# One-hot blocks of layers 0 and 3 on ScalarE, one counter step per tile's sum, a third bank for layer 3's queries, and groups of one tile at a layer's end

## What is computed

```python
# layer 0 (four heads of 64; layer 2 alike, without elu; layer 1 one head, returns h + att @ node)
Wh = (h @ W).reshape(n, heads, d)
e  = leaky_relu(s_i[:, None, :] + s_j[None, :, :], 0.2)     # s_i, s_j: Wh times two halves of a
e  = where((adj == 0)[:, :, None], -inf, e)
out = elu(einsum('ijh,jhd->ihd', softmax(e, axis=1), Wh))
# layer 3 (attention with q, k, v)
scores = einsum('hnd,hmd->hnm', q, k) / 8 + (edge.T - 1) * 10000
ctx = einsum('hnm,hmd->hnd', softmax(scores, axis=-1), v)
```

## Time and profile before

| | us |
|---|---|
| median of 3 runs | 2181.08 (2172.83 to 2183.22) |
| the profiled execution | 2191.25 |
| span of the profile | 2189.4 |
| first part, to layer 0's gathers | 272 |
| layer 0, first gather to layer 1's first | 272 to 778 |
| layer 1 | 778 to 1244 |
| layer 2 | 1244 to 1712 |
| layer 3 | 1712 to 2189 |

### The profile page before, as it was taken

One profiled execution on the slowest core, in us unless ns is written; L12 is line 12 of the kernel. 1 busy time (PEld: TensorE's weight loads), 2 busy tenths in 40 slices (PEclk: granted clock), 3 DMA queues, 4 the chain that ended last, 5 costly groups with the idle time before them and its releaser, 6 DMA issues.

```text
span 2189.4 us, 24682 instructions
## 1 busy us (share of the span) xinstructions
PE 1404.7 (64%) x8310; PEld 1025.4 (47%) x8310; DVE 1550.8 (71%) x3408; ACT 577.5 (26%) x1038; POOL 1294.8 (59%) x1299
## 2 busy tenths in 40 slices
PE   3655223676676625666767437777888477777776
PEld 2434122555555414444555334554555265655565
DVE  3768897888888735555565256766776388888887
ACT  6777350222222201222222102222222111111111
POOL 0000077777776067777776277777772577777771
PEclk9555556778778758878788568988889789888988
DMA  9997134444443034444443134444542577777771
GB/s 374 404 366 249 14 99 118 113 120 116 116 115 100 15 93 108 112 112 112 112 111 100 51 105 128 139 138 136 138 138 87 182 225 226 218 212 212 216 216 58
DMA packets 151027, 328.57 MB, mean 150 GB/s; under 512 B 31210, under 2 KB 62832, under 8 KB 150896
## 3 DMA queue, kind: packets, MB, share of 16 engines
q0 software_dynamic: 71680, 213.24, 35.8%
q1 hardware_dynamic: 61552, 92.57, 11.7%
q10 hardware_dynamic: 17664, 21.12, 2.8%
HBM read 294.93 MB, written 31.90 MB: 149 GB/s over the span
## 4 chain that ended last, share of the span: by engine, by line
POOL 31%; DVE 24%; PE 19%; issue 16%; ACT 6%; DMA 2%; SPq 1%; ACTq 0%; DVEq 0%; POOLq 0%
POOL s_gb L749 31%; PE ps L1691 8%; DVE s_gb L1428 6%; PE ps L1607 4%; PE ps L1645 3%; DVE s_F L1366 2%; DVE s_F L1364 2%; ACT s_a L781 2%; DVE s_ST L1252 2%; DVE s_S L1407 2%; PE ps L1656 1%; DVE s_sc L1352 1%; PE ps L1589 1%; DMA s_adj<-in_adj_dram 1%; DVE s_tmp L1348 1%
## 5 line engine op out<-in xcount | busy, mean ns | idle before, releaser
L749 POOL DMA_INDIRECT s_gb<-s_tab,s_ji x1280 | 1290.6, 1008 | 600.2 <-issue 384.7
L1691 PE MATMUL ps<-s_gb,s_S 128*128 128x260 f32 (+1 forms) x2560 | 704.0, 435 | 30.5 <-DVE s_gb L1428 23.7
L1691 PEld LDWEIGHTS ps<-s_gb,s_S 128*128 128x128 f32 x2560 | 552.2, 222 | 132.0 <-DVE s_gb L1428 26.2
L1428 DVE TENSOR_TENSOR s_gb<-s_gb,ps 128x1024 f32<-128x1024 f32 (+1 forms) x288 | 291.4, 1035 | 1.2 <-ACT ps L946 1.2
L1607 PE MATMUL ps<-s_wx,s_hT 128*128 128x264 f32 (+2 forms) x512 | 224.9, 575 | 83.7 <-ACT s_tb L887 42.7
L1656 PE MATMUL ps<-s_ident,s_sc 128*16 128x128 f32 (+1 forms) x384 | 79.6, 367 | 230.4 <-DVE s_sc L1327 229.6
L1645 PE MATMUL ps<-s_qs,s_ST 128*128 128x256 bf16 x960 | 156.9, 328 | 43.4 <-DVE s_tmp L1348 29.5
L1607 PEld LDWEIGHTS ps<-s_wx,s_hT 128*128 128x128 f32 x512 | 111.9, 242 | 147.0 <-ACT s_tb L887 49.8
L1322 DVE TENSOR_TENSOR s_sc<-s_sc,s_gb 128x80 f32<-128x80 f32 (+1 forms) x48 | 10.9, 227 | 210.6 <-DMA s_gb<-s_tab,s_ji 208.2
L1656 PEld LDWEIGHTS ps<-s_ident,s_sc 128*16 128x16 f32 (+1 forms) x384 | 39.7, 111 | 255.9 <-DVE s_sc L1327 238.3
L1364 DVE TENSOR_TENSOR_SCAN s_F<-s_d,ps 16x768 f32<-16x768 bf16 (+1 forms) x64 | 111.4, 1741 | 60.8 <-PE ps L1656 60.0
(11 more groups left out here) (190 smaller groups left out, 1622.8 us busy)
## 6 DMA issues: line engine op xcount, KB each, us to landing
s_adj<-in_adj_dram SPq DMA_DIRECT2D x32, 2048.0 KB, 14.4
s_gb<-s_tab,s_ji POOLq DMA_INDIRECT x1280, 3.0
s_tab<-s_tb ACTq DMA_DIRECT2D x32, 260.0 KB, 3.7
s_tab<-s_tb ACTq DMA_DIRECT2D x32, 256.0 KB, 4.2
s_q<-s_qs SPq DMA_DIRECT2D x16, 384.0 KB, 3.1
s_qs<-s_q SPq DMA_DIRECT2D x32, 192.0 KB, 4.2
s_tab<-s_tb ACTq DMA_DIRECT2D x16, 257.0 KB, 3.6
s_xs<-in_x_dram SPq DMA_DIRECT2D x8, 512.0 KB, 14.4
```

The source lines that it names most:

```text
L749: e.indirect_dma_start(gb[:, 0, k, :], None, self.tab_d[L.n], bass.IndirectOffsetOnAxis(ap=self.idx[:, t, k:k + 1], axis=0)).then_inc(self ...
L1428: e.tensor_tensor(vv[:, k0:k1], vv[:, k0:k1], wide(p[:, k0:k1, :], 3, L.hd), ALU.mult).then_inc(self.weighed)
L1691: m = e.matmul(o, self.S[:, z, i, :], g4[:, 0, k, lo:lo + o.shape[1]], start=(k == 0), stop=(k == KT - 1))
```

## The change

Five things are changed.

1. **One-hot blocks of layers 0 and 3 on ScalarE** (`act_onehot`). For each block one activation computes `(irel - count)^2` (`Square`, bias `irel`, a column of 128 values), ten for a tile; then three activations make `max(0, 1 - 4 * that)` (`Relu`), over 4, 4 and 2 blocks. VectorE's L1407 is gone from layer 0, and `pe_stage` and `act_stage` from layer 3.
2. **`S` holds two whole tiles**, ten blocks each (the last two of them in `qs` or behind the ring in `gb`), and `agg` is raised once for a tile, behind its last block.
3. **Three banks** (0, 6, 7) for layer 3's expanded queries. TensorE runs 18 expansions ahead at the start instead of 17, does two between the sums instead of three, and three ahead of `pe_turn` instead of two.
4. **17 groups**: tiles 30 and 31 are groups 15 and 16 of one tile each, in the attention and in the next table. `tiles(n)` and `group(t)` replace the pairs.
5. **A new order of each layer's end**, written out for all engines from group 14 on, with one extra exponential of one element (`act_exp_table`) that loads the activation table.

Groups 0 to 13 of layers 0 to 2 keep their order, but for the one-hot blocks.

```diff
+    def tiles(self, n):
+        return (2 * n, 2 * n + 1) if n < 15 else (n + 15,)
+    def group(self, t):
+        return t // 2 if t < 30 else t - 15
...
+    def act_onehot(self, e, L, t):
+        g = T * L.n + t
+        if t == 0 and L.n == 0:
+            e.wait_ge(self.lists_out, 16)
+        if g >= 2:
+            e.wait_ge(self.agg, g - 1)
+        for U in range(3 * g, 3 * g + 3):
+            many, k0 = self.many(U)
+            for i in range(many):
+                m = e.activation(self.s_part(U)[:, i, :], self.count[:], ACT.Square,
+                                 bias=self.irel[:, t, k0 + i:k0 + i + 1], scale=-1.0)
+            m.then_inc(self.apart)
+        for U in range(3 * g, 3 * g + 3):
+            e.wait_ge(self.apart, (U if L.n == 0 else U - 6 * T) + 1)
+            e.activation(self.s_part(U), self.s_part(U), ACT.Relu, bias=self.ones[:, 0:1], scale=-4.0).then_inc(self.S_ok)
+    def act_exp_table(self, e):
+        e.activation(self.idle[:], self.ones[0:1, 0:1], ACT.Exp)
...
     def act_layer(self, e, L, lo, hi):
...
             if L.n == 0:
+                self.act_onehot(e, L, 2 * n)
                 self.act_exp_elu(e, 2 * n)
...
+            if L.n == 0:
+                self.act_onehot(e, L, 2 * n + 1)
...
+        self.act_hidden(e, l, 13)
...
+        self.act_rows(e, l, 13)
...
+            self.act_onehot(e, L, 28)
+            self.act_onehot(e, L, 29)
+            self.act_exp_elu(e, 28)
+            self.act_exp_elu(e, 29)
+        self.act_root(e, l, 14)
+        self.act_exp_table(e)
+        self.act_hidden(e, l, 14)
+        self.act_turned(e, l, 14)
+        self.act_exp(e, L, 15)
+        self.act_rows(e, l, 14)
...
+        if L.n == 0:
+            self.act_onehot(e, L, 30)
+            self.act_exp_elu(e, 30)
+        self.act_exp(e, L, 16)
...
+        self.act_root(e, l, 15)
+        if L.n == 0:
+            self.act_onehot(e, L, 31)
...
     def vec_layer(self, e, L, lo, hi):
...
+        self.vec_norm(e, l, 13)
+        if L.n == 2:
+            self.vec_r(e, 12)
+        self.vec_spread(e, L, 14)
...
+        self.vec_scores(e, L, 15)
+        self.vec_shift(e, L, 15)
...
+        self.vec_spread(e, L, 15)
+        own(e, 13)
+        self.vec_scores(e, L, 16)
...
+        self.vec_shift(e, L, 16)
+        self.vec_done(e, L, 30)
+        self.vec_var(e, l, 15)
+        self.vec_spread(e, L, 16)
...
     def pe_expand_q(self, e, x):
...
-        if x >= 2:
-            e.wait_ge(self.q_mul, x - 1)
+        if x >= 3:
+            e.wait_ge(self.q_mul, x - 2)
...
     def pe_layer(self, e, L, lo, hi):
...
+        self.pe_expand(e, L, 15)
+        self.pe_hidden(e, l, 13)
+        self.pe_table(e, l, 13)
+        self.pe_tile(e, L, 28)
+        self.pe_tile(e, L, 29)
+        self.pe_turn(e, L, 15)
+        self.pe_hidden(e, l, 14)
+        self.pe_turn_back(e, L, 15)
+        self.pe_expand(e, L, 16)
+        self.pe_table(e, l, 14)
+        self.pe_tile(e, L, 30)
+        self.pe_turn(e, L, 16)
+        self.pe_turn_back(e, L, 16)
+        self.pe_tile(e, L, 31)
+        self.pe_hidden(e, l, 15)
+        self.pe_project(e, l, 15)
+        self.pe_hidden(e, l, 16)
+        if L.n == 2:
+            self.pe_q(e, 15)
+        self.pe_table(e, l, 16)
```

706 lines of the change are left out of this document (388 added, 318 removed).

## The result

The changed kernel takes 2301.27 us (median of 4 runs, 2296.81 to 2301.72) against 2180.32 before (2172.83 to 2183.22): ratio 1.0556, 95% interval 1.0526 to 1.0585. The forecast was 2238 and its range ended at 2278; the direction was right, and the loss is twice what I had.

The account below looks back on a forecast made before the run. The prediction took no engine as full, so the order of the queues bounds the kernel; +31 + 21 + 11 + 11 - 17 = +57 on the 2181.08 us median gave 2238 us, range 2155 to 2278.

Parts of the forecast that it names:

- Layer 0, steady: Layer 0's steady groups: sums wait for ScalarE's one-hots, cycle 25.19 to 27.6 us, +31 us over thirteen groups.
- it ends at 9.75: Layer 0's cycle: the sum of tile 2n starts at +3.75 us after ScalarE's last copy and ends at 9.75.
- it ends at 21.3: Layer 0's cycle: the sum of tile 2n+1 has its first blocks at 15.9 us and ends at 21.3.
- The slow bound: Layer 0's steady groups with Squares at 0.40 us each: cycle 29.6 to 30.5 us, +57 to +69 us.
- No engine is full: Layer 0, groups 1 to 13: VectorE 86% busy, POOL 76%, TensorE 70%, ScalarE 25%, so the order of the queues counts.
- A: Whole kernel, the forecast case: slower, 2238 us, own range 2200 to 2275, chance 0.66.
- Rival B: Whole kernel faster, 2125 us: one-hots never late, VectorE relieved of 3.0 to 3.6 us a group, layer 0 -39; chance 0.19.
- End of layer 0: Layer 0's last groups: two serial shifts between sums and two exposed one-hot tiles, +21 us, bounds +13 to +28.
- Layer 1: Layer 1's end, where only the order changes: table 13 goes first (+8.3), +11 us in all, from +5 to +13.
- End of layer 2: Layer 2's end: +11 us, from +5 to +14, with one more wait, for the copy of group 12's queries.
- The same walk: Layer 2's end taken step by step like layer 1's, ending at 1723.1 us against 1712.07.
- Layer 3: Layer 3 without stages and with a third bank: 27.72 to 26.4 us a group, -17 us, from -24 to 0.

Follow-up runs that it names:

- ends_b: Changed kernel with sums of tiles 28 and 29 ahead of table 13 in layers 1 and 2, layer 2's query copy later; 2791.46 us against 2773.40 for before.
- b_l3: Kernel before with only layer 3's part of the change; 2737.12 us against 2773.40 once, 2695.60 against 2721.54 in several runs, ratio 0.9902.
- l0_early: Changed kernel with layer 0's one-hot tiles one place earlier in ScalarE's queue; 2770.03 us against 2801.46 for before, repeat in several runs ratio 1.0072.
- warm_gaps2: Changed kernel with six unread matmuls ahead of each sum of layer 0, second run; 2764.91 us against 2706.69 for before.

## Why the prediction was wrong, step by step

- **Layer 0, steady: +68.8 instead of +31.** The queue was read right and the Squares priced right (0.294 us, 0.30 taken). The step that failed is in "it ends at 9.75" and "it ends at 21.3": I took the sums at 6.0 and 5.4 us from the earlier trace rows, which TensorE had needed in a cycle with a mean clock of 0.79, for a cycle into which I had just put two waits. They took 7.5 us each, 5.8 of them at the low clock. Against my walk the cycle has +0.6 at the start of the first sum, +1.5 in it, +2.1 in the second, +0.1 between, and -1.1 in the tail: 27.6 becomes 30.7. Over all thirteen steps, the first of which are shorter, that is 38 us more than forecast. The slow bound (+69) held this number by luck: I had put it on the Squares. The runs with filled pauses show the clock's part.
- **"No engine is full"** was misread: POOL's 76% leave out the 0.30 us between its issues, which I counted in layer 3. With them it was taken up nearly whole, and only its lead kept it from bounding layer 0. The forecast for A didn't rest on it, B did.
- **End of layer 0: +27.3 instead of +21**, inside its bounds. 20 of it are one-hots, the rest order.
- **Layer 1: +7.9 instead of +11.** Its end is +10.7, as forecast, and table 13 ahead of the sums, the cause that I named, is worth 8 us of it. That the sum came out so well is in part luck: the end that it is measured against ran at a mean clock of 0.71, and the same code needed 62.5 us instead of 70.8 on a chip where it had 0.83.
- **End of layer 2: +24.4 instead of +11.** "The same walk" failed: a table of layer 2 with its queries keeps TensorE 11.8 us (1760.96 to 1772.78, its projections at the low clock), one of layer 1 7.1 (1280.72 to 1287.82), and I carried layer 1's over, twice, which makes an estimated 9. Of the waits, `vec_r(12)`, which I named, stood beside table 13 here; the one that cost was `act_q0(13)`, with `act_root(14)` behind it, some 3.3 us. `ends_b` shows 4.2 for the first table's place; the other's is argued.
- **Layer 3: -19.9 instead of -17**, with 26.3 us a group for 26.4, and POOL as the bound, as forecast. How the gain on this chip divides between the stages and the bank is not shown.
- **First part: +3.5.** I had nothing here, and its cause is open. In the other runs with the change layer 0's gathers start at 272.5 to 274.7 us (275.6 here), in `b_l3` at 271.9 and 271.4 (272.1 before).
- **From the profiled execution to the median: 10.** The profiled execution of before was 10.9 us over its median, that of after (2301.06) stood at its own. I carried the offset over. 53 us of terms and these 10 are the 63 by which 2301 misses 2238.
- **The range** ended at 2278, the forecast with slow Squares alone; the upper bounds of all terms together (69, 28, 13, 14 and 0) would have made 2305, and held the result. None of them stood for a clock that falls in steady groups; I had named the low clock only for the ends. At the lower end, 2159 counts the ends at 15, while their lower bounds add up to 23.
- **Rival B** counted VectorE's relief as layer 0's gain. `l0_early` has the relief and no waits, and its step is 22 us, so where nothing else bounds it the relief is worth 3 us a group, as B had it. On the first chip B's 39 us would have put group 14's second scan at 667, ahead of the issue of tile 29's last gather at 674: at POOL's pace B could not have given them in any order.

## What to carry to other kernels

When a change puts a wait ahead of TensorE, price its matmuls anew: each duration in a trace holds only at the clock of its own stretch (here 4.6 to 7.5 us for one and the same sum), so find rows of the same instructions in a stretch with such pauses and use those. When work moves to an idle engine, ask where in that engine's queue it stands and what it stands behind; an engine that was 25% busy delayed both sums of every group by being asked late, and one place earlier cost the groups nothing. An engine whose row says 76% may be full: look at what lies between its instructions. A walk made for one layer may be used for the next only with that layer's own lengths, and a step measured on one chip is compared with the same step of the old code on that chip.

## What the runs showed of the hardware that I had not expected

- The same ten-block sum took 4.6 us at a granted clock of 1.00 (`warm_gaps2`) and 7.5 with 5.8 us of it at 0.50 (after); two dozen useless matmul instructions in the step from group 13 to 14 shortened it by 2.6 and 5.8 us.
- The same code of layer 1's end took 70.8 us at a mean clock of 0.71 (before) and 62.5 at 0.83 (`b_l3`).
- On five other chips the gathers of the same kernels landed so late that before took 2700 to 2800 us instead of 2180. On one of them the change that costs 5.6% on the first chip cost 2.1%.
